# An encoder layer in fp32: z's transpose moved from TensorE to a trip through DRAM and 32x32 blocks on VectorE

## What is computed

```
q = (x @ Wq + bq) / 4;  k = ctx @ Wk + bk;  v = ctx @ Wv + bv      # per head of 16
p = softmax over keys j < i of q k^T (query 0 gets all zeros)
a = concat(p v) @ Wo + bo
z = layer_norm(x + a, ln1_g, ln1_b)
out = layer_norm(z + relu(z @ W1 + b1) @ W2 + b2, ln2_g, ln2_b)
```

## Time and profile before

| | us |
|---|---|
| median of 3 runs (1674.67 to 1674.99) | 1674.93 |
| time of the profiled execution | 1674.59 |
| its span | 1672.8 |
| PE busy in the span | 1613.9 (96%) |
| ACT busy | 1538.7 (92%) |
| DVE busy | 1444.6 (86%) |
| POOL busy | 1385.1 (83%) |
| all DMAs, share of 16 engines | 59.1% |

### The profile page before, as it was taken

One profiled execution on the slowest core, in us unless ns is written; L12 is line 12 of the kernel. 1 busy time (PEld: TensorE's weight loads), 2 busy tenths in 40 slices (PEclk: granted clock), 3 DMA queues, 4 the chain that ended last, 5 costly groups with the idle time before them and its releaser, 6 DMA issues.

```text
span 1672.8 us, 54026 instructions
## 1 busy us (share of the span) xinstructions
PE 1613.9 (96%) x16672; PEld 1588.0 (95%) x16672; DVE 1444.6 (86%) x6744; ACT 1538.7 (92%) x5889; POOL 1385.1 (83%) x1358
## 2 busy tenths in 40 slices
PE   2699999999999999999999999999999999999997
PEld 2689999999999999999999999999999999999996
DVE  5688988988988898898898898898898898889874
ACT  1789999999999999999999999999999999999993
POOL 2368888888888888888888888888888888888896
PEclk9789999999999999999999999999999999999999
DMA  7756656556656656656665656665665665665520
GB/s 163 143 109 130 134 119 132 137 121 132 130 127 127 133 127 126 129 133 122 129 134 120 134 133 116 135 135 118 134 134 121 134 133 124 126 133 126 116 60 27
DMA packets 307071, 208.99 MB, mean 125 GB/s; under 512 B 164320, under 2 KB 281952, under 8 KB 306784
## 3 DMA queue, kind: packets, MB, share of 16 engines
q1 hardware_dynamic: 306784, 205.52, 59.1%
HBM read 104.73 MB, written 50.33 MB: 93 GB/s over the span
## 4 chain that ended last, share of the span: by engine, by line
PE 94%; SPq 2%; ACT 1%; DVE 1%; issue 1%; POOL 1%; DMA 1%; POOLq 0%; ACTq 0%; DVEq 0%
PE ps_dense L356 32%; PE ps_dense L366 32%; PE ps_probsT L461 14%; PE ps_scores L451 7%; PE ps_att L475 7%; PE ps_dense L339 2%; ACT probs L528 1%; SPq L245 0%; SPq L229 0%; DMA k_stack<-k_spill 0%; SPq L285 0%; SPq L223 0%; POOL hT L926 0%; SPq L312 0%; SPq L289 0%
## 5 line engine op out<-in xcount | busy, mean ns | idle before, releaser
L528 ACT ACTIVATE probs<-ps_scores,negmax 128x128 f32<-128x128 f32 x2048 | 741.9, 411 | 12.8 <-DVE negmax L697 9.1
L918 POOL TENSOR_TENSOR probs<-probs,recip 128x512 f32<-128x512 f32 x512 | 531.5, 1038 | 153.4 <-DVE recip L691 153.4
L697 DVE CUSTOM_DVE_ANT_0 ps_scores<-ps_scores,mask 128x128 f32<-128x128 f32 x2048 | 528.4, 320 | 78.3 <-PE ps_scores L451 76.0
L528 ACT ACTIVATION_READ_ACCUMULATOR probs<-ps_scores,negmax 128x1 f32 x2048 | 516.8, 252 | 0.0
L366 PE MATMUL ps_dense<-w,hT 128*128 128x256 f32 x3072 | 420.9, 286 | 1.7 <-DVE u L826 0.9
L356 PE MATMUL ps_dense<-zT,w 128*128 128x256 f32 x3072 | 416.9, 285 | 0.5 <-DVE h_f L789 0.5
L926 POOL TENSOR_TENSOR hT<-h_f,hT 128x512 fp32r<-128x512 f32 x256 | 326.4, 1284 | 93.5 <-DVE h_f L789 93.5
L356 PEld LDWEIGHTS ps_dense<-zT,w 128*128 128x128 f32 x3072 | 381.8, 189 | 0.9 <-issue 0.9
L366 PEld LDWEIGHTS ps_dense<-w,hT 128*128 128x128 f32 x3072 | 380.3, 188 | 2.3 <-issue 1.2
L540 ACT ACTIVATE probsT<-ps_probsT 128x508 f32<-128x508 f32 x512 | 318.6, 622 | 37.0 <-PE ps_probsT L461 37.0
L461 PE MATMUL ps_probsT<-ident,probs 128*128 128x128 f32 x2048 | 313.9, 276 | 0.0
(11 more groups left out here) (75 smaller groups left out, 2332.6 us busy)
## 6 DMA issues: line engine op xcount, KB each, us to landing
q_stack<-qT SPq DMA_DIRECT2D x768, 64.0 KB, 2.0
k_stack<-k_spill SPq DMA_DIRECT2D x384, 128.0 KB, 4.3
k_spill<-kT SPq DMA_DIRECT2D x128, 256.0 KB, 2.2
x_tok<-in_x_dram SPq DMA_DIRECT2D x256, 64.0 KB, 2.4
c_tok<-in_ctx_dram SPq DMA_DIRECT2D x256, 64.0 KB, 4.8
x_res<-in_x_dram SPq DMA_DIRECT2D x64, 256.0 KB, 3.1
out_dram<-o_tok SPq DMA_DIRECT2D x64, 256.0 KB, 2.6
probsT<-in_L_xattn_W_dram SPq DMA_DIRECT2D x1, 1024.0 KB, 5.6
```

The lines of the kernel that those rows point to most:

```text
L528: last = nc.scalar.activation(probs[:, m % 4, i, :], ps_scores[m % 2][:, i, :], ACT.Exp, bias=negmax[:, m % 4, i:i + 1], scale=-1.0, accum ...
L697: last = nc.vector.tensor_tensor_reduce(ps_scores[m % 2][:, i, :], ps_scores[m % 2][:, i, :], mask[:], -1.0, -MASKED, ALU.add, ALU.min, ac ...
L918: nc.gpsimd.tensor_tensor(probs[:, m % 4], probs[:, m % 4], recip[:, m % 4, :].unsqueeze(2).broadcast_to([P, 4, S]), ALU.mult)\
```

## The change

z leaves PE. `spill_z` (SP) writes the standardised `u1` to DRAM in one DMA of 256 KB; `load_z` waits for that DMA and for `norm1_sum`, and reads z back in four DMAs of 64 KB into `x_res`, one for each quadrant of 32 partitions. DVE transposes it there in place by 32x32 blocks (`z_flips`); `z_hi` and `z_lo` read the tile in place of a PSUM bank. `load_residual`, which fills the same tile, has to wait for `z_lo` of the group before (before: for `norm1_sum` of that group). The rows of W1, and the columns ln1_g and ln1_b, are loaded in the feature order that this gives, in four DMAs each in place of one. PSUM's banks are dealt out anew, and the five lists of calls are written in other orders, with some stages an iteration later; the loops run over one more iteration. The same numbers are computed.

The diff, without most of the lists of calls:

```diff
-ITERATIONS = range(-5, NG + 6)
-BANK = {"zT": 2, "v": 0, "q": 2, "f1_0": 2, "k": 0, "f1_1": 1, "f1_2": 2, "f1_3": 0, "wo": 1, "f2": 1}
+ITERATIONS = range(-6, NG + 6)
+BANK = {"v": 0, "q": 1, "f1_0": 2, "k": 2, "f1_1": 0, "f1_2": 1, "f1_3": 2, "wo": 2, "f2": 1}
...
+        z_dram = nc.dram_tensor("z_spill", (2, GB, S, D), F32).ap()
+        z_blocks = z_dram.rearrange("g b (o t) (j n) -> g j t (b o) n", t=32, j=4)
...
+        z_tile = x_res[:].rearrange("p b d -> p (b d)").rearrange("p (o k) -> p o k", k=KC * 32)
+
+        def z_by_chunk():
+            return z_tile.rearrange("p o (c t) -> p c o t", c=KC)
...
-        COLS = [(bq, bq_col), (bk, bk_col), (b1, b1_col), (ln1_g, g1_col), (ln1_b, be1_col)]
+        COLS = [(bq, bq_col), (bk, bk_col), (b1, b1_col)]
+        BLOCK_COLS = [(ln1_g, g1_col), (ln1_b, be1_col)]
+        ALL_COLS = len(COLS) + 4 * len(BLOCK_COLS)
+        BLOCK_ROWS = (0, 1, 2, 4)
...
             def load_residual(g):
                 if exists(g):
-                    need(sp, taken["wo"], g)
+                    need(sp, s_zlo, g)
                     sp.dma_start(x_res[:], x_v[g]).then_inc(s_xres, 16)
+
+            def spill_z(g):
+                if exists(g):
+                    sp.wait_ge(s_z1, GB * (g + 1))
+                    need(sp, s_zrow, 16 * 4 * (g - 1))
+                    sp.dma_start(z_dram[g % 2].rearrange("b s d -> s b d"), u1[:]).then_inc(s_zspill, 16)
+
+            def load_z(g):
+                if exists(g):
+                    sp.wait_ge(s_zspill, 16 * (g + 1))
+                    sp.wait_ge(taken["wo"], g + 1)
+                    for j in range(4):
+                        sp.dma_start(z_tile[32 * j:32 * j + 32], z_blocks[g % 2, j]).then_inc(s_zrow, 16)
...
-            def z_transpose(g):
-                if exists(g):
-                    pe.wait_ge(s_z1, GB * (g + 1))
-                    transposes(g, "zT", u1)
...
             def ff_up(g, n):
                 if exists(g):
-                    pe.wait_ge(taken["zT"], g + 1)
+                    pe.wait_ge(s_zlo, g + 1)
...
             def z_hi(g):
                 if exists(g):
-                    take_hi("zT", zT, g, full["f1_3"], g)
+                    act.wait_ge(s_zflip, g + 1)
+                    need(act, full["f1_3"], g)
+                    nc.scalar.activation(zT[:, 0].rearrange("p c (o t) -> p c o t", t=32), z_by_chunk(), ACT.Copy)\
+                      .then_inc(s_hi["zT"], 1)
...
+            def z_flips(g):
+                if exists(g):
+                    dve.wait_ge(s_zrow, 16 * 4 * (g + 1))
+                    nc.vector.transpose(z_tile, z_tile).then_inc(s_zflip, 1)
+
             def z_lo(g):
                 if exists(g):
-                    take_lo("zT", zT, g)
+                    dve.wait_ge(s_hi["zT"], g + 1)
+                    nc.vector.tensor_tensor(zT[:, 1].rearrange("p c (o t) -> p c o t", t=32), z_by_chunk(),
+                                            f32(zT[:, 0]).rearrange("p c (o t) -> p c o t", t=32), ALU.subtract)\
+                      .then_inc(s_zlo, 1)
...
-                    need(dve, full["zT"], g)
+                    need(dve, s_zspill, 16 * g)
...
-                k_project(it + 1)
-                scores(it, 3)
-                ff_up(it - 2, 1)
+                k_project(it + 1)
+                probs_transpose(it - 1, 7)
+                scores(it, 3)
```

More of the change, by code:

```diff
@@ L308, in _ @@
                 sp.dma_start(tile[:], dram.rearrange("(c p) -> p c", p=P), allow_slow_non_contiguous=True).then_inc(s_wc, 16)
+            for dram, tile in BLOCK_COLS:
+                by_block = dram.rearrange("(j c d) -> j d c", j=4, c=KC)
+                for j in range(4):
+                    sp.dma_start(tile[32 * j:32 * j + 32], by_block[j], allow_slow_non_contiguous=True).then_inc(s_wc, 16)
             for i in range(2, 5):
@@ L333, in bank_free @@
                     pe.wait_ge(taken[prev], (g + 1) * TAKES.get(prev, 1))
[L335 to L342, removed]
             def weights_split(g, n):
@@ L540, in take_probsT @@
                 nc.scalar.activation(probsT[:, (g * UNITS + m) % NPT, :, 1:S], ps_probsT[m % 2][:, :, 1:S], ACT.Copy).then_inc(s_pTsb, 1)
-            def take_hi(name, dst, g, reader, done):
-                act.wait_ge(full[name], g + 1)
-                need(act, reader, done)
-                nc.scalar.activation(dst[:, 0].rearrange("p c t -> p (c t)"), ps_dense[BANK[name]][:], ACT.Copy)\
-                  .then_inc(s_hi[name], 1)
             def round_hi(dst, flip, g, s_flip, s_done, reader, done):
@@ L621, in iteration @@
             def iteration(it):
-                k_hi(it + 1)
-                take_probsT(it - 1, 7)
+                take_probsT(it, 0)
+                att_hi(it - 1)
+                exponentials(it, 4)
+                h_hi(it - 2, 0)
+                take_probsT(it, 1)
+                q_hi(it + 2)
+                exponentials(it, 5)
                 h_hi(it - 2, 1)
-                exponentials(it, 3)
+                x_hi(it + 3)
+                take_probsT(it, 2)
+                exponentials(it, 6)
                 h_hi(it - 2, 2)
-                att_hi(it - 1)
-                take_probsT(it, 0)
-                exponentials(it, 4)
+                take_probsT(it, 3)
+                norm1(it - 1)
+                exponentials(it, 7)
                 h_hi(it - 2, 3)
-                take_probsT(it, 1)
-                exponentials(it, 5)
-                norm2(it - 3)
-                take_probsT(it, 2)
-                q_hi(it + 2)
-                exponentials(it, 6)
-                c_hi(it + 2)
-                norm1(it - 1)
-                take_probsT(it, 3)
-                exponentials(it, 7)
-                z_hi(it - 1)
-                x_hi(it + 3)
-                take_probsT(it, 4)
+                take_probsT(it, 4)
+                c_hi(it + 2)
                 exponentials(it + 1, 0)
@@ L646, in iteration @@
                 exponentials(it + 1, 1)
-                h_hi(it - 1, 0)
                 take_probsT(it, 6)
+                k_hi(it + 2)
                 exponentials(it + 1, 2)
+                take_probsT(it, 7)
+                norm2(it - 3)
+                z_hi(it - 1)
+                exponentials(it + 1, 3)
             for it in ITERATIONS:
@@ L977, in iteration @@
             def iteration(it):
[L978 to L980 removed]
+                rstd2(it - 5)
+                normalise(it - 1, 1)
+                scale_z2(it - 5)
+                normalise(it - 1, 2)
                 offset_z2(it - 5)
[L982 removed]
                 scale_z1(it - 3)
[L984 removed]
+                normalise(it - 1, 3)
+                residual(it - 2)
                 h_lo(it - 3, 0)
[L986 to L987 removed]
+                normalise(it - 1, 4)
+                normalise(it - 1, 5)
+                rstd1(it - 2)
                 h_lo(it - 3, 1)
[L989 to L991 removed]
+                offset_z1(it - 3)
+                normalise(it - 1, 6)
                 h_lo(it - 3, 2)
+                normalise(it - 1, 7)
                 h_lo(it - 3, 3)
[L994 to L996 removed]
+                normalise(it, 0)
             for it in ITERATIONS:
```

130 lines of the change are left out of this document (59 added, 71 removed).

## The result

The changed kernel takes 1729.96 us (median of 4 runs, 1728.45 to 1734.62) against 1674.89 us: a ratio of 1.0336, 95% interval 1.0323 to 1.0349. The prediction was slower, 1698 us with a range to 1722: the sign was right, and the size, +23 us against +55, was too small by more than half.

The account below looks back on a forecast made before the run. PE was taken to bound the kernel before, the loop over k after: 1674.59 + 15 (loop) + 8 (fill and drain) = 1697.6 us profiled, 0.34 more against the median: 1698 us, range 1658 to 1722.

Parts of the forecast that it names:

- the landing: In the loop over k, from k_stack's first issue until its last DMA is down: 7.8 us.
- the loop over k: Scores through K, z_lo, residual load, ctx and k_stack DMAs to next scores: period 25.1 us, +15 us, chance 0.53.
- the fill: Program start: nine more DMAs ahead of the first groups' loads and ctx's four ahead of k_stack, +5 us.
- the end: Drain: z's trip through DRAM near 7.5 us in place of 0.6, partly covered by three product blocks, +3 us.
- PE's part: PE's list per group falls from 24.86 to 24.43 us without z's transposes; 24.5 was taken.
- K full: In the loop over k, PE finishes k's projection 9.05 us after scores(it, 0).
- the price of `z_lo`: DVE's z_lo in the loop over k, partly waiting for POOL's scale_z2: 1.2 us, between 0.7 and 1.5.
- issue with its pauses: SP in the loop over k: residual 0.63 us, ctx's four 1.97, plus 0.25 for pauses.
- rival 4: DVE's z_lo waits for all that is left of POOL's scale_z2: loop 25.4 us, 1716 us in all, chance 0.13.
- The leverage: Loop over k between 23.25 us, where PE bounds (-22 us), and 26.4 (+94 us), over 61 steady groups.
- DVE at 23.2 us a group: DVE's work with z's transpose and z_lo's SBUF reads added: 22.2 + 1.0 us, in a group of 24.5.
- rival 2: ACT's chain before the next scores(it, 1) sets the period: near 24.7 us, 1674 us in all, chance 0.11.

Follow-up runs that it names:

- f4: Kernel before the change with one of z's four transposes on PE left in place of four: 1655.48 us, ratio 0.9885.
- h1: Changed kernel with SP's order alone altered: k_stack (hi part first) ahead of ctx's loads, then the next x ahead of q_stack: 1684.09 us, ratio 1.0076.
- f2: e2 without z's spill and load; DVE transposes u1 directly, so z's features are in another order than W1's rows: 1683.84 us, ratio 1.0061.
- h4: e2 with DVE's norm2_moments moved behind c_lo, nothing else: 1687.78 us, ratio 1.0080.
- g2: e2 with DVE's x_lo moved from behind c_lo to ahead of reciprocals(it, 1): 1696.10 us, ratio 1.0130.
- h3: h1 with norm2_moments behind c_lo, x_lo ahead of reciprocals(it, 1) and z in its own tile: 1677.39 us, ratio 1.0018.
- e1: Changed kernel with the six k_stack DMAs ahead of both the residual's load and ctx's four loads: 2032.45 us, ratio 1.2121.
- e2: Changed kernel with ctx's four loads issued behind the six k_stack DMAs, the residual's load still ahead: 1689.95 us, ratio 1.0102.

## Why the prediction was wrong in size

Four terms of the sum were too small: `z_lo` and the landing in the loop over k, the fill, and the end. The loop was priced at +15 us and measured at +36.8, fill and end at +8 and measured at +19.0.

**PE's part was right.** In the changed kernels PE's list without waits is 24.33 us, the sum of the least time that each item took; 24.43 was worked out. f4 confirms the worth of a transpose.

**The loop over k was the right mechanism.** By its steps, as means over 54 groups after, predicted in brackets: K full 8.95 (9.05), `z_lo` done 14.70 (14.4), k_stack's first issue 17.39 (17.05 + 0.25), landing 7.98 (7.8), then 0.10 till scores (nothing): 25.47 (25.1). The first step that failed is the price of `z_lo`: "I take 1.2, nearest to that row". It is 1.36 in every group and begins 0.14 us later, together 0.30; landing and the last 0.10 make another 0.28, and issue with its pauses was priced 0.21 too high (0.05 of it a slip: 14.4 + 0.63 + 1.97 is 17.00, not 17.05). That is rival 4, priced at 25.4, which had 0.13 of the loop's 0.53. DVE and POOL hold each other up to the end of the instruction: the rule of the Trainium skill (SBUF — State Buffer, section "SBUF: two separate sides"); by that rule, the trace agrees: 1.36 against 0.69 us alone, though `z_lo` ends 0.55 us behind `scale_z2` and not the full 0.69.

**The leverage was seen but not the size.** 0.37 us more a group are 22 of the 32 us missed. When a loop only just misses the bound, each tenth of a microsecond counts 61 times.

**Fill and drain, +8, were +19.** That step failed too. The fill is SP's queue, as said, but +9.0 rather than +5: the first groups' own loads, in their new order, are as much of it as the nine new DMAs, as h1 shows, which gains 5 us there by order alone. At the end the trip was priced, and the wrong thing was priced: f2, without any trip, ends 76.0 us after the last scores(it, 0), before 67.5. PE's timeline at the end, before and then after:

```profile
1638.79 1.69 PE L356 MATMUL ps_dense<-zT,w 128*128 128x256 f32 x12
1640.32 1.70 PE L366 MATMUL ps_dense<-wo,aT 128*128 128x256 f32 x12
1642.92 3.11 PE L366 MATMUL ps_dense<-w,hT 128*128 128x256 f32 x24 [0.90 <-DVE u L826]
```

```profile
1690.43 1.68 PE L391 MATMUL ps_dense<-wo,aT 128*128 128x256 f32 x12 [0.51 <-DVE h_f L806]
1691.94 3.00 PE L381 MATMUL ps_dense<-zT,w 128*128 128x256 f32 x24
1696.60 3.08 PE L391 MATMUL ps_dense<-w,hT 128*128 128x256 f32 x24 [1.65 <-POOL hT L944]
1700.31 3.08 PE L391 MATMUL ps_dense<-w,hT 128*128 128x256 f32 x24 [0.64 <-POOL hT L944]
1704.02 5.95 PE L381 MATMUL ps_dense<-zT,w 128*128 128x256 f32 x48 [0.62 <-DVE zT L756]
```

To hide the trip, `ff_up` and `ff_down` moved some 10 us later in the list. With nothing behind them they come out at the end: the last wo block starts 39.3 us after the last scores(it, 0) in place of 35.0. Two `ff_up` blocks of the group before (3.00 us) stand behind it that stood ahead of it, and PE's waits from there on add up to 5.7 us in place of 2.6. So the depth that was added to the pipeline is paid for when it empties.

**DVE at 23.2 us a group** came out at 24.0 with its waits on POOL, and it mattered only in part: c_lo's lateness cost little (h4), the rest of that time lay where nobody waited (g2).

**What is left: rival 2's chain.** In the middle, from 210 to 1575 us, a group takes 24.67 us in h3 (24.87 before), 0.34 over PE's 24.33. Half of that, 0.17, is ahead of scores(it, 1). The timelines of ACT and PE in h3 show it:

```profile
864.82 0.21 ACT L548 ACTIVATION_READ_ACCUMULATOR probs<-ps_scores,negmax 128x1 f32 x1
```

```profile
865.17 0.48 PE L472 MATMUL ps_scores<-k_stack,q_stack 96*128 96x256 f32 x2
```

These scores start 0.14 us after the end of ACT's last exponentials of the group before, whose place they take, and so they do in all 47 of 55 groups in which they start late. That is the chain of rival 2, which had its limit at 24.7. Another 0.10 is ahead of scores(it, 0); in 14 of the 55 groups k_stack's last DMA lands just before. No run shortened ACT's chain, so what it would give is open.

## What to carry to other kernels

When work leaves the fullest engine, price the loops that the change closes, instruction by instruction, and take for a two-tile DVE instruction beside a POOL one the price to POOL's end: where a loop misses the bound by half a microsecond, that choice decides. Count the issue time of the DMA queue as an engine of its own: it has a list, it fills up, and taking away the wait ahead of it gains only as far as its next one. And when stages are moved later to hide a latency, charge the move itself to the end of the kernel, whether or not the latency is hidden.

## What the hardware showed that I had not expected

- An instruction of DVE on two tiles of SBUF and one of POOL delay each other both ways: xT's low part 1.78 us beside POOL, 0.68 apart (g2), and POOL's h_lo 1.67 in place of 1.28.
- Where PE waited in every group, 3.8 us on average and up to 6.0 (e1), the granted clock of the middle was 0.92: behind most of these waits it was at the lower of the two levels, 1.2 in place of 2.4 GHz. With waits of at most 2.6 us, as after, the clock of the same stretch was 1.00.
- A wait row names the DMA that lands nearest to its end; with several transfers in flight that was the wrong one.
- In the runs with a higher DMA share k_stack lands later: 7.98 us for its six after (DMA share 0.64), 8.2 in e2 (0.71), 8.9 in h1 to h3 (0.75 to 0.78). The order of the DMAs differs between them too, and no run separates the two.
